# The last group of an encoder layer: low parts on VectorE, the second norm and the store batch by batch

## The chip, the core and the metric

The kernel runs on one core of one Trainium2 chip. The metric is the device time of a whole execution in microseconds, as the median of several runs. In the profile the engines are PE (TensorE, matmuls), PEld (its weight loads), DVE (VectorE), ACT (ScalarE), POOL (GpSimd) and SP (SyncE, which here only issues DMAs).

## What is computed

One transformer layer with cross attention, in float32, over 128 sequences of 128 tokens and 256 features:

```python
q, k, v = x @ Wq + bq, ctx @ Wk + bk, ctx @ Wv + bv        # 16 heads of 16
scores  = where(j < i, q k^T / 4, -1e30)
attn    = softmax(scores); attn[query 0] = 0
x   = layer_norm(x + (attn v) @ Wo + bo, ln1_g, ln1_b)
out = layer_norm(x + relu(x @ W1 + b1) @ W2 + b2, ln2_g, ln2_b)   # W1: 256 x 1024, W2: 1024 x 256
```

## The kernel before

The 128 sequences are worked off in 64 groups of two (`NG` = 64, `GB` = 2), so a group has 256 tokens; the last one is group 63. Each float32 operand of a dense product is kept as two `float32r` parts: a high part, which ScalarE rounds off while it takes the result out of PSUM, and a low part, the float32 value less the high part. A product is then three matmuls (`SPLIT`: high by high, high by low, low by high) into one PSUM bank.

Every engine runs a program written by hand: a function `iteration(it)` lists its steps, and each step carries the group that it belongs to at that point (`h_lo(it - 3, 0)`). It is called for `it` from -5 to 69, so several groups are in work at once, and steps of groups that don't exist fall away (`exists`). Engines meet only in semaphores; within an engine the order is the order of the code. Nothing else plans the work.

In the last iterations only the feed-forward half of group 63 is left. It goes as follows.

- TensorE, `ff_up(g, n)` for n = 0 to 3 (lines 439 to 443, `columns_product`, line 377): 12 matmuls each, giving 256 of the 1024 hidden features. The matmuls of n = 2 use the PSUM bank of n = 0 and wait until VectorE has taken that.
- ScalarE, `h_hi(g, n)` (line 660): relu with bias, rounded, into `hT[:, 0]`, in two instructions.
- VectorE, `h_full(g, n)` (line 866): the same relu in full float32 into `h_f32[:, n % 2]`, also in two instructions. It waits until the low part of n - 2 has been made, as there are two buffers.
- GpSimd, `h_lo(g, n)` (line 1014): `hT[:, 1]` = `h_f32` - `hT[:, 0]`, 128x512.
- TensorE, `ff_down(g, q)` for q = 0 to 3 (lines 445 to 457, `tokens_product`, line 387): 12 matmuls each; q = 0 and 1 are batches 0 and 1 over the first four chunks of hidden features, q = 2 and 3 over the last four. Both batches lie in one bank (`f2`, 512 columns). The first half waits for the low parts of n = 0 and 1, the second for 2 and 3.
- VectorE, `norm2_sum` (line 920, result plus `y_b2`, the residual), `norm2_stats` (line 882), `norm2_moments` (lines 888 to 892: mean and variance, `var_eps`, `neg_mean`).
- GpSimd, `rstd2` (lines 1050 and 1052): the reciprocal root and the offset, on two columns.
- ScalarE, `norm2` (line 678, in `standardise`): `u2 * rstd + offset`, one instruction per batch.
- GpSimd, `scale_z2` (line 1058, times the row `g2_row`, which waits for both batches) and `offset_z2` (line 1063, plus `be2_row`), both 128x512 in `o_tok`.
- SyncE, `store` (line 291): one DMA of 256 KB per group.

`y_b2` of group 63 is made by GpSimd in `scale_z1` (line 1037) and `offset_z1` (line 1044). In GpSimd's last iterations these steps stand between others of group 62: `rstd2` and `scale_z2` of group 62, `offset_z1` of 63, `offset_z2` of 62, `rstd2` of 63.

Of the kernel before, what the change touches and what calls it, by code (L numbers as in the profile page):

```python
# [7 lines left out]
ALU = mybir.AluOpType  # L8
# [31 lines left out]
def exists(g):  # L40

    return 0 <= g < NG
# [8 lines left out]
def encoder_layer(nc, x, ctx_in, Wq, bq, Wk, bk, Wv, bv, Wo, bo, ln1_g, ln1_b, W1, b1, W2, b2, ln2_g, ln2_b, out):  # L51
    ctx = ExitStack()
    with ctx:
# [138 lines left out]
        s_o = sem("o_ready")  # L192
        s_out = sem("out_stored")

        def f32(ap):

            return ap.bitcast(F32)

        WEIGHTS = [(Wq, wq, KC, D), (Wk, wk, KC, D), (Wv, wv, KC, D), (Wo, wo, KC, D), (W1, w1, KC, FF),
# [30 lines left out]
        def _(sp):  # L230
# [57 lines left out]
            def store(g):  # L288
                if exists(g):
                    sp.wait_ge(s_o, g + 1)  # L290
                    sp.dma_start(out_v[g], o_tok[:]).then_inc(s_out, 16)
# [41 lines left out]
            for it in ITERATIONS:  # L333
                iteration(it)
            sp.wait_ge(s_out, 16 * NG)


        @block.tensor
        def _(pe):
# [41 lines left out]

            def tokens_product(name, w, acts, b, kcs, total, starts=True):


                for kc in kcs:
                    for n, (a, c) in enumerate(SPLIT):
                        last = nc.tensor.matmul(ps_dense[BANK[name]][:, b * D:(b + 1) * D],  # L387
                                                acts[:, a, kc, b * S:(b + 1) * S], w[:, c, kc, :],
                                                start=(starts and kc == 0 and n == 0),
                                                stop=(kc == total - 1 and n == len(SPLIT) - 1),  # L390
                                                skip_group_check=True)
                return last
# [52 lines left out]
            def ff_down(g, q):  # L445
                if exists(g):
                    if q == 0:
                        weights_split(g, 5)
                        bank_free(g, "f2")
                    b, half = q % 2, q // 2  # L450
                    if b == 0:
                        pe.wait_ge(s_hlo[2 * half], g + 1)
                        pe.wait_ge(s_hlo[2 * half + 1], g + 1)
                    last = tokens_product("f2", w2, hT, b, range(4 * half, 4 * half + 4), FC,
                                          starts=(b == 0))
                    if q == 3:
                        last.then_inc(full["f2"], 1)
# [274 lines left out]
        def _(dve):  # L732
# [123 lines left out]
            def h_full(g, n):  # L856
                if exists(g):
# [7 lines left out]
                    for i in range(2):  # L865
                        last = nc.vector.tensor_scalar(  # L866
                            h_f32[:, n % 2, i, :], ps_dense[BANK[f"f1_{n}"]][:, i * GT:(i + 1) * GT],
                            b1_col[:, 2 * n + i:2 * n + i + 1], 0.0, ALU.add, ALU.max)
                    last.then_inc(taken[f"f1_{n}"], 1)

            def att_lo(g):
# [39 lines left out]
            def norm1_moments(g):  # L911
                if exists(g):
                    moments(0, g, s_st1, s_mv1, s_ve1, s_of1)

            def norm2_sum(g):
                if exists(g):
                    dve.wait_ge(full["f2"], g + 1)
# [6 lines left out]
            def norm2_stats(g):  # L924
                if exists(g):
                    statistics(1, u2, g, taken["f2"], s_st2)
# [52 lines left out]
            for it in ITERATIONS:  # L979
                iteration(it)  # L980


        @block.gpsimd
        def _(pool):
# [25 lines left out]
            def h_lo(g, n):  # L1010
                if exists(g):
                    pool.wait_ge(taken[f"f1_{n}"], g + 1)
# [41 lines left out]
            def scale_z2(g):  # L1054
                if exists(g):
                    pool.wait_ge(s_z2, GB * (g + 1))
                    need(pool, s_out, 16 * g)
                    nc.gpsimd.tensor_tensor(o_tok[:], u2[:], row(g2_row), ALU.mult).then_inc(s_og, 1)

            def offset_z2(g):  # L1060
                if exists(g):
                    pool.wait_ge(s_og, g + 1)
# [52 lines left out]
```

## Time and profile before

| | us |
|---|---|
| median of 3 runs (lowest, highest) | 1667.87 (1667.69, 1668.47) |
| the profiled execution | 1669.3 |
| its span in the trace | 1667.4 |
| busy in the span: PE | 1619.5 (97%) |
| PEld | 1592.4 (95%) |
| ACT | 1549.0 (93%) |
| DVE | 1432.2 (86%) |
| POOL | 1386.5 (83%) |

TensorE is busy nearly all the time. The groups repeat with a period of some 25 us, and the profile's picture in 40 slices shows full slices for all engines but the first and the last. In the last slice PE falls to 7 tenths, VectorE to 4 and ScalarE to 3. How the last stretch runs is read from the rows further down.

### The profile page before, as it was taken

The numbers are of one execution on the slowest core, as the hardware profiler recorded it, in microseconds if no ns is written. First come the engines' busy times: TensorE is split into PE (matmuls) and PEld (weight loads), VectorE is DVE, ScalarE is ACT, GpSimd is POOL, SyncE is SP. The second block draws the span as 40 slices with busy tenths as digits, with TensorE's granted clock in tenths as the row PEclk, the third lists the DMA queues.
The fourth block names the chain that finished last, engine by engine and source line by source line (L and its number), as shares of the span: only waits on it lengthen the run. The fifth ranks groups of instructions, "written<-read, shape, count | busy, mean of one in ns | idle before, by whom it ended". The sixth has DMA issues, their size and how long they took to land.

```text
span 1667.4 us, 54091 instructions
## 1 busy us (share of the span) xinstructions
PE 1619.5 (97%) x16700; PEld 1592.4 (95%) x16700; DVE 1432.2 (86%) x6735; ACT 1549.0 (93%) x5907; POOL 1386.5 (83%) x1358
## 2 busy tenths in 40 slices
PE   4799999999999999999999999999999999999997
PEld 3699999999999999999999999999999999999996
DVE  3688898898898898898898898898898889889874
ACT  3799999999999999999999999999999999999993
POOL 2368888888888888888888888888888888888896
PEclk7799999999999999999999999999999999999999
DMA  7856656656666655665665665665665665665520
GB/s 146 174 118 123 131 134 121 131 126 127 133 135 116 135 133 117 136 134 120 132 137 117 132 134 121 135 131 126 127 134 126 128 130 128 127 130 130 112 60 27
DMA packets 307071, 208.99 MB, mean 125 GB/s; under 512 B 164320, under 2 KB 281952, under 8 KB 306784
## 3 DMA queue, kind: packets, MB, share of 16 engines
q1 hardware_dynamic: 305088, 204.60, 59.6%
q8 instruction: 136, 2.23, 0.6%
q14 instruction: 151, 1.24, 0.3%
q10 hardware_dynamic: 1696, 0.92, 0.3%
HBM read 104.73 MB, written 50.33 MB: 93 GB/s over the span
## 4 chain that ended last, share of the span: by engine, by line
PE 94%; DMA 1%; SPq 1%; DVE 1%; ACT 1%; issue 1%; POOL 1%; POOLq 0%; ACTq 0%; DVEq 0%
PE ps_dense L377 32%; PE ps_dense L387 32%; PE ps_probsT L480 14%; PE ps_scores L470 7%; PE ps_att L498 7%; PE ps_dense L359 2%; ACT probs L575 0%; DMA k_spill<-kT 0%; SPq L278 0%; DMA k_stack<-k_spill 0%; POOL hT L1014 0%; DMA probs<-in_L_xattn_Wk_dram 0%; SPq L235 0%; DMA q_stack<-qT 0%; SPq L241 0%
## 5 line engine op out<-in xcount | busy, mean ns | idle before, releaser
L575 ACT ACTIVATE probs<-ps_scores,negmax 128x128 f32<-128x128 f32 x2048 | 744.2, 413 | 8.4 <-DVE negmax L782 5.0
L1006 POOL TENSOR_TENSOR probs<-probs,recip 128x512 f32<-128x512 f32 x512 | 534.2, 1044 | 136.7 <-DVE recip L765 136.5
L782 DVE CUSTOM_DVE_ANT_0 ps_scores<-ps_scores,mask 128x128 f32<-128x128 f32 x2048 | 527.6, 319 | 71.8 <-PE ps_scores L470 69.6
L575 ACT ACTIVATION_READ_ACCUMULATOR probs<-ps_scores,negmax 128x1 f32 x2048 | 517.4, 253 | 0.0
L387 PE MATMUL ps_dense<-w,hT 128*128 128x256 f32 x3072 | 420.9, 286 | 1.8 <-DVE u L903 0.9
L377 PE MATMUL ps_dense<-zT,w 128*128 128x256 f32 x3072 | 416.9, 285 | 0.5 <-DVE h_f L866 0.5
L1014 POOL TENSOR_TENSOR hT<-h_f,hT 128x512 fp32r<-128x512 f32 x256 | 327.6, 1294 | 93.3 <-DVE h_f L866 93.3
L377 PEld LDWEIGHTS ps_dense<-zT,w 128*128 128x128 f32 x3072 | 381.8, 189 | 0.9 <-issue 0.9
L387 PEld LDWEIGHTS ps_dense<-w,hT 128*128 128x128 f32 x3072 | 380.3, 188 | 2.3 <-issue 1.2
L592 ACT ACTIVATE probsT<-ps_probsT 128x508 f32<-128x508 f32 x512 | 319.2, 623 | 40.3 <-PE ps_probsT L480 40.1
L480 PE MATMUL ps_probsT<-ident,probs 128*128 128x128 f32 x2048 | 314.9, 276 | 0.0
L782 DVE DVE_READ_ACCUMULATOR2_ANT negmax<- 128x1 f32 x2048 | 287.1, 140 | 0.0
L480 PEld LDWEIGHTS ps_probsT<-ident,probs 128*128 128x128 f32 x2048 | 237.6, 141 | 12.7 <-issue 12.7
L470 PE MATMUL ps_scores<-k_stack,q_stack 96*128 96x256 f32 x1024 | 211.4, 288 | 21.9 <-ACT probs L575 14.1
L660 ACT ACTIVATE hT<-ps_dense,b_col 128x256 fp32r<-128x256 f32 x512 | 219.1, 492 | 13.7 <-PE ps_dense L377 9.9
L866 DVE TENSOR_SCALAR h_f<-ps_dense,b_col 128x256 f32<-128x256 f32 x512 | 222.9, 476 | 9.0 <-ACT hT L660 5.5
L470 PEld LDWEIGHTS ps_scores<-k_stack,q_stack 96*128 96x128 f32 x1024 | 161.0, 193 | 24.7 <-ACT probs L575 14.4
L678 ACT ACTIVATE u<-u,offset,rstd 128x256 f32<-128x256 f32 x256 | 150.2, 683 | 11.6 <-POOL offset L1052 8.2
L498 PE MATMUL ps_att<-probsT,v_sb 128*32 128x128 f32 x4096 | 126.8, 276 | 0.4 <-ACT probsT L592 0.4
L498 PEld LDWEIGHTS ps_att<-probsT,v_sb 128*32 128x32 f32 x4096 | 109.1, 111 | 9.4 <-ACT probsT L592 0.7
L377 PE MATMUL ps_dense<-xT,wq 128*128 128x256 f32 x756 | 104.8, 289 | 7.1 <-DVE xT L810 7.1
L1044 POOL TENSOR_TENSOR y_b<-y_b,be_row 128x512 f32<-128x512 f32 x64 | 108.8, 1700 | 0.0
(84 smaller groups left out, 2335.3 us busy)
## 6 DMA issues: line engine op xcount, KB each, us to landing
k_stack<-k_spill SPq DMA_DIRECT2D x384, 128.0 KB, 4.4
q_stack<-qT SPq DMA_DIRECT2D x762, 64.0 KB, 2.0
k_spill<-kT SPq DMA_DIRECT2D x128, 256.0 KB, 2.2
c_tok<-in_ctx_dram SPq DMA_DIRECT2D x256, 64.0 KB, 4.8
x_res<-in_x_dram SPq DMA_DIRECT2D x64, 256.0 KB, 3.1
out_dram<-o_tok SPq DMA_DIRECT2D x64, 256.0 KB, 2.8
x_tok<-in_x_dram SPq DMA_DIRECT2D x252, 64.0 KB, 2.4
probsT<-in_L_xattn_W_dram SPq DMA_DIRECT2D x1, 1024.0 KB, 11.1
```

The costliest lines, as they stand in the source:

```text
L377: last = nc.tensor.matmul(bank_of(name, g)[:, i * GT:(i + 1) * GT], w[:, a, kc, ch * P:(ch + 1) * P], acts[:, c, kc, :], start=(n == 0), s ...
L387: last = nc.tensor.matmul(ps_dense[BANK[name]][:, b * D:(b + 1) * D], acts[:, a, kc, b * S:(b + 1) * S], w[:, c, kc, :], start=(starts and ...
L470: last = nc.tensor.matmul(bank[:, 2 * i:2 * i + 2, :], q_stack[g % 2][:, j, c, b * S:(b + 1) * S], k_stack[g % 2][:, 4 * c + j, :, b * S:( ...
L480: last = nc.tensor.transpose(ps_probsT[m % 2][:, i, :], probs[:, m % 4, i, :], ident[:])
L498: last = nc.tensor.matmul(ps_att[32 * j:32 * j + 32, (c * GB + b) * S:(c * GB + b + 1) * S], v_sb[g % 2][:, b, 4 * c + j, e:e + 2, :], pro ...
L575: last = nc.scalar.activation(probs[:, m % 4, i, :], ps_scores[m % 2][:, i, :], ACT.Exp, bias=negmax[:, m % 4, i:i + 1], scale=-1.0, accum ...
L592: nc.scalar.activation(probsT[:, (g * UNITS + m) % NPT, :, 1:S], ps_probsT[m % 2][:, :, 1:S], ACT.Copy).then_inc(s_pTsb, 1)
L660: last = nc.scalar.activation(hT[:, 0, 2 * n + i, :], ps_dense[BANK[f"f1_{n}"]][:, i * GT:(i + 1) * GT], ACT.Relu, bias=b1_col[:, 2 * n + ...
L782: last = nc.vector.tensor_tensor_reduce(ps_scores[m % 2][:, i, :], ps_scores[m % 2][:, i, :], mask[:], -1.0, -MASKED, ALU.add, ALU.min, ac ...
L866: last = nc.vector.tensor_scalar(h_f32[:, n % 2, i, :], ps_dense[BANK[f"f1_{n}"]][:, i * GT:(i + 1) * GT], b1_col[:, 2 * n + i:2 * n + i + ...
L1006: nc.gpsimd.tensor_tensor(probs[:, m % 4], probs[:, m % 4], recip[:, m % 4, :].unsqueeze(2).broadcast_to([P, 4, S]), ALU.mult)\
L1014: nc.gpsimd.tensor_tensor(hT[:, 1, 2 * n:2 * n + 2, :], h_f32[:, n % 2], f32(hT[:, 0, 2 * n:2 * n + 2, :]), ALU.subtract).then_inc(s_hlo[n ...
```

## The change

Everything is tied to the last group (`g == NG - 1`); the other 63 are as before.

- `h_lo` of group 63 is dropped from GpSimd. In its place VectorE makes each low part right behind its `h_full`, after a wait on its own result (`taken[f1_n]`).
- The down product of batch 1 goes to a bank that the scores no longer need (`last_half`, the first half of `ps_scores[0]`); batch 0 stays. The order of the matmuls is unchanged. When batch 0 is complete (q = 2), a semaphore tells so.
- `last_sum` takes the place of `norm2_sum` and `norm2_stats`: sum and statistics of batch 0 on its own semaphore, then those of batch 1.
- `scale_z2` and `offset_z2` of group 63 are dropped from GpSimd. `last_out`, VectorE's last step, does both for each batch as that batch leaves ScalarE, again with a wait on its own result between the two.
- The store of group 63 is two DMAs of 128 KB, one per batch.

```diff
+        last_half = ps_scores[0][:, 0:2].rearrange("p h k -> p (h k)")
...
             def store(g):
-                if exists(g):
+                if g == NG - 1:
+                    for b in range(GB):
+                        sp.wait_ge(s_o, NG + b)
+                        sp.dma_start(out_v[g][:, b], o_tok[:, b]).then_inc(s_out, 16)
+                elif exists(g):
                     sp.wait_ge(s_o, g + 1)
                     sp.dma_start(out_v[g], o_tok[:]).then_inc(s_out, 16)
...
                     last = tokens_product("f2", w2, hT, b, range(4 * half, 4 * half + 4), FC,
-                                          starts=(b == 0))
+                                          starts=(b == 0 or g == NG - 1),
+                                          home=last_half if g == NG - 1 and b == 1 else None)
+                    if q == 2 and g == NG - 1:
+                        last.then_inc(s_first_half, 1)
...
                     last.then_inc(taken[f"f1_{n}"], 1)
+                    if g == NG - 1:
+                        dve.wait_ge(taken[f"f1_{n}"], g + 1)
+                        nc.vector.tensor_tensor(hT[:, 1, 2 * n:2 * n + 2, :], h_f32[:, n % 2],
+                                                f32(hT[:, 0, 2 * n:2 * n + 2, :]), ALU.subtract).then_inc(s_hlo[n], 1)
...
+            def last_sum():
+                g = NG - 1
+                dve.wait_ge(s_yb, g + 1)
+                need(dve, s_og, g)
+                for b, (s_full, count) in enumerate(((s_first_half, 1), (full["f2"], g + 1))):
+                    dve.wait_ge(s_full, count)
+                    nc.vector.tensor_tensor(u2[:, b, :], last_half if b else ps_dense[BANK["f2"]][:, 0:D], y_b2[:, b, :],
+                                            ALU.add).then_inc(s_sum0, 1)
+                    dve.wait_ge(s_sum0, b + 1)
+                    nc.vector.bn_stats(stats[:, 1, b, :], u2[:, b, :]).then_inc(s_st2, 1)
+
+            def last_out():
+                g = NG - 1
+                need(dve, s_out, 16 * g)
+                for b in range(GB):
+                    dve.wait_ge(s_z2, GB * g + b + 1)
+                    nc.vector.tensor_tensor(o_tok[:, b, :], u2[:, b, :], g2_row[:], ALU.mult).then_inc(s_last, 1)
+                    dve.wait_ge(s_last, b + 1)
+                    nc.vector.tensor_tensor(o_tok[:, b, :], o_tok[:, b, :], be2_row[:], ALU.add).then_inc(s_o, 1)
...
             def h_lo(g, n):
-                if exists(g):
+                if exists(g) and g < NG - 1:
...
             def scale_z2(g):
-                if exists(g):
+                if exists(g) and g < NG - 1:
...
             def offset_z2(g):
-                if exists(g):
+                if exists(g) and g < NG - 1:
```

What this moves is shown at three places. The rows name line, operation, output, inputs and shape, and in brackets the semaphores waited for (`h0_lo` is the low part of n = 0, `h0_hi` its high part, `f1_0_taken` the end of `h_f32` of n = 0). The line numbers of the changed kernel are higher. First VectorE in the up projection of group 63, from the moments of group 62 on, before:

```order
L888 BN_AGGR mv<-stats 128x2 [waits stats2_ready]
L888 BN_AGGR mv<-stats 128x2
L891 TENSOR_SCALAR var_eps<-mv 128x2 [waits offset2_ready,meanvar2_ready]
L892 TENSOR_SCALAR neg_mean<-mv 128x2
L866 TENSOR_SCALAR h_f<-ps_dense,b_col 128x256 [waits h3_lo,h1_hi]
L866 TENSOR_SCALAR h_f<-ps_dense,b_col 128x256
L866 TENSOR_SCALAR h_f<-ps_dense,b_col 128x256 [waits h0_lo,h2_hi]
L866 TENSOR_SCALAR h_f<-ps_dense,b_col 128x256
L866 TENSOR_SCALAR h_f<-ps_dense,b_col 128x256 [waits h1_lo,h3_hi]
L866 TENSOR_SCALAR h_f<-ps_dense,b_col 128x256
```

The same place after, from the moments' `var_eps` on:

```order
L905 BN_AGGR mv<-stats 128x2
L908 TENSOR_SCALAR var_eps<-mv 128x2 [waits offset2_ready,meanvar2_ready]
L909 TENSOR_SCALAR neg_mean<-mv 128x2
L879 TENSOR_SCALAR h_f<-ps_dense,b_col 128x256 [waits h3_lo,h1_hi]
L879 TENSOR_SCALAR h_f<-ps_dense,b_col 128x256
L885 TENSOR_TENSOR hT<-h_f,hT 128x512 [waits f1_1_taken]
L879 TENSOR_SCALAR h_f<-ps_dense,b_col 128x256 [waits h0_lo,h2_hi]
L879 TENSOR_SCALAR h_f<-ps_dense,b_col 128x256
L885 TENSOR_TENSOR hT<-h_f,hT 128x512 [waits f1_2_taken]
L879 TENSOR_SCALAR h_f<-ps_dense,b_col 128x256 [waits h1_lo,h3_hi]
L879 TENSOR_SCALAR h_f<-ps_dense,b_col 128x256
L885 TENSOR_TENSOR hT<-h_f,hT 128x512 [waits f1_3_taken]
```

A subtraction of 128x512 now follows each pair of relu instructions, and the next pair stands behind it.

Then VectorE from the down product of group 63 to its end, before:

```order
L920 TENSOR_TENSOR u<-ps_dense,y_b 128x512 [waits z2_scaled,y_b2_ready,f2_full]
L882 BN_STATS stats<-u 128x6 [waits f2_taken]
L882 BN_STATS stats<-u 128x6
L888 BN_AGGR mv<-stats 128x2 [waits stats2_ready]
L888 BN_AGGR mv<-stats 128x2
L891 TENSOR_SCALAR var_eps<-mv 128x2 [waits offset2_ready,meanvar2_ready]
L892 TENSOR_SCALAR neg_mean<-mv 128x2
```

and after:

```order
L938 TENSOR_TENSOR u<-ps_dense,y_b 128x256 [waits last_f2_first_batch_full,z2_scaled,y_b2_ready]
L941 BN_STATS stats<-u 128x6 [waits last_sum_first_batch]
L938 TENSOR_TENSOR u<-ps_scores,y_b 128x256 [waits f2_full]
L941 BN_STATS stats<-u 128x6 [waits last_sum_first_batch]
L905 BN_AGGR mv<-stats 128x2 [waits stats2_ready]
L905 BN_AGGR mv<-stats 128x2
L908 TENSOR_SCALAR var_eps<-mv 128x2 [waits offset2_ready,meanvar2_ready]
L909 TENSOR_SCALAR neg_mean<-mv 128x2
L948 TENSOR_TENSOR o_tok<-u,g_row 128x256 [waits z2_ready,out_stored]
L950 TENSOR_TENSOR o_tok<-o_tok,be_row 128x256 [waits last_scaled]
L948 TENSOR_TENSOR o_tok<-u,g_row 128x256 [waits z2_ready]
L950 TENSOR_TENSOR o_tok<-o_tok,be_row 128x256 [waits last_scaled]
```

One sum of 128x512 has become two of 128x256, each with its statistics, and four instructions with the rows stand at the end.

Last GpSimd from the second `h_lo` of group 63 to its end, before:

```order
L1014 TENSOR_TENSOR hT<-h_f,hT 128x512 [waits f2_full,f1_1_taken]
L1050 TENSOR_TENSOR rstd<-var_eps,neg_half 128x2 [waits z2_ready,var_eps2_ready]
L1052 TENSOR_TENSOR offset<-neg_mean,rstd 128x2 [waits rstd2_ready]
L1014 TENSOR_TENSOR hT<-h_f,hT 128x512 [waits f2_full,f1_2_taken]
L1014 TENSOR_TENSOR hT<-h_f,hT 128x512 [waits f2_full,f1_3_taken]
L1058 TENSOR_TENSOR o_tok<-u,g_row 128x512 [waits out_stored,z2_ready]
L1044 TENSOR_TENSOR y_b<-y_b,be_row 128x512 [waits z1_scaled]
L1063 TENSOR_TENSOR o_tok<-o_tok,be_row 128x512 [waits z2_scaled]
L1050 TENSOR_TENSOR rstd<-var_eps,neg_half 128x2 [waits z2_ready,var_eps2_ready]
L1052 TENSOR_TENSOR offset<-neg_mean,rstd 128x2 [waits rstd2_ready]
L1058 TENSOR_TENSOR o_tok<-u,g_row 128x512 [waits out_stored,z2_ready]
L1063 TENSOR_TENSOR o_tok<-o_tok,be_row 128x512 [waits z2_scaled]
```

and after, from the residual's scale (`y_b`) on:

```order
L1077 TENSOR_TENSOR y_b<-u,g_row 128x512 [waits f2_taken,z1_ready]
L1090 TENSOR_TENSOR rstd<-var_eps,neg_half 128x2 [waits z2_ready,var_eps2_ready]
L1092 TENSOR_TENSOR offset<-neg_mean,rstd 128x2 [waits rstd2_ready]
L1098 TENSOR_TENSOR o_tok<-u,g_row 128x512 [waits out_stored,z2_ready]
L1084 TENSOR_TENSOR y_b<-y_b,be_row 128x512 [waits z1_scaled]
L1103 TENSOR_TENSOR o_tok<-o_tok,be_row 128x512 [waits z2_scaled]
L1090 TENSOR_TENSOR rstd<-var_eps,neg_half 128x2 [waits z2_ready,var_eps2_ready]
L1092 TENSOR_TENSOR offset<-neg_mean,rstd 128x2 [waits rstd2_ready]
```

Between `rstd` of group 62 and `o_tok` of group 62 no `hT` is left, and behind the last `rstd` and `offset` nothing is.

## Rows read from the trace of the kernel before

**Rows 1.** Stretches: us, busy PE, PEld, DVE, ACT, POOL (instructions), PEclk, DMA share, GB/s.

```profile
1652.00:1658.00 6.00, 5.60 (x46) 5.23 (x44) 0.72 (x3) 1.09 (x2) 5.97 (x6) 1.00 0.02 4
...
1662.00:1663.00 1.00, 0.00 (x0) 0.00 (x0) 0.00 (x0) 0.20 (x1) 0.72 (x1) 0.50 0.00 0
```

**Rows 2.** Timeline, TensorE: start us, length us, line, operation, count, [idle before, releaser].

```profile
1641.39 3.10 PE L387 MATMUL ps_dense<-w,hT 128*128 128x256 f32 x24
1644.32 3.00 PE L377 MATMUL ps_dense<-zT,w 128*128 128x256 f32 x24
1647.84 3.08 PE L377 MATMUL ps_dense<-zT,w 128*128 128x256 f32 x24 [0.52 <-DVE h_f L866]
1651.44 3.08 PE L387 MATMUL ps_dense<-w,hT 128*128 128x256 f32 x24 [0.52 <-POOL hT L1014]
1654.86 3.09 PE L387 MATMUL ps_dense<-w,hT 128*128 128x256 f32 x24 [0.35 <-POOL hT L1014]
```

**Rows 3.** Timeline, GpSimd, the last group.

```profile
1647.77 1.29 POOL L1014 TENSOR_TENSOR hT<-h_f,hT 128x512 fp32r<-128x512 f32 x1 [1.13 <-DVE h_f L866]
...
1652.18 2.54 POOL L1014 TENSOR_TENSOR hT<-h_f,hT 128x512 fp32r<-128x512 f32 x2
1654.66 1.29 POOL L1058 TENSOR_TENSOR o_tok<-u,g_row 128x512 f32<-128x512 f32 x1
```

**Rows 4.** Timeline, VectorE, the same stretch.

```profile
1646.82 0.88 DVE L866 TENSOR_SCALAR h_f<-ps_dense,b_col 128x256 f32<-128x256 f32 x2 [0.82 <-ACT hT L660]
...
1647.88 1.20 DVE L891 TENSOR_SCALAR var_eps<-mv 128x2 f32<-128x2 f32 x1
...
1650.41 0.87 DVE L866 TENSOR_SCALAR h_f<-ps_dense,b_col 128x256 f32<-128x256 f32 x2 [0.48 <-ACT hT L660]
1651.83 0.88 DVE L866 TENSOR_SCALAR h_f<-ps_dense,b_col 128x256 f32<-128x256 f32 x2 [0.55 <-ACT hT L660]
```

**Rows 5.** The chain of waits behind the last matmul: start us, length us, what.

```profile
1657.98 0.70 DVE u L920
...
1658.71 0.77 DVE stats L882 x2
...
1661.11 0.60 ACT u L678
1661.71 0.50 ACTq L53
...
1662.28 1.26 POOL o_tok L1058
...
1663.58 1.30 POOLq L53
```

**Rows 6.** DMA from 1664 to 1668: GB/s in slices of 0.1 us; KB, us to landing.

```profile
GB/s 0 0 0 0 0 0 0 0 0 0 0 0 0 0 0 0 0 10 287 369 379 420 358 399 318 82 0 0 0 0 0 0 0 0 0 0 0 0 0 0
...
out_dram<-o_tok SPq DMA_DIRECT2D x1, 256.0 KB, 2.1
```

**Rows 7.** Groups by form, VectorE: shapes, count, busy us, mean ns.

```profile
L748 DVE TENSOR_TENSOR w<-o_tok,w 128x512 fp32r<-128x512 f32 x1 | 0.7, 678 | 0.0
...
L753 DVE TENSOR_TENSOR b_col<-ps_att,b_col 128x8 f32<-128x8 f32 x1 | 0.2, 166 | 1.4 <-PE ps_att L400 1.4
```

**Rows 8.** Timeline, VectorE and GpSimd around 1578 us.

```profile
1577.71 1.58 DVE L810 TENSOR_TENSOR cT<-c_flip,cT 128x512 fp32r<-128x512 f32 x1
...
1577.45 1.29 POOL L1044 TENSOR_TENSOR y_b<-y_b,be_row 128x512 f32<-128x512 f32 x1
1578.70 1.74 POOL L1063 TENSOR_TENSOR o_tok<-o_tok,be_row 128x512 f32<-128x512 f32 x1
```

**Rows 9.** Timeline, ScalarE, the last two groups.

```profile
1635.06 0.84 ACT L660 ACTIVATE hT<-ps_dense,b_col 128x256 fp32r<-128x256 f32 x2 [0.99 <-PE ps_dense L377]
1635.79 1.08 ACT L678 ACTIVATE u<-u,offset,rstd 128x256 f32<-128x256 f32 x2
...
1650.96 0.84 ACT L660 ACTIVATE hT<-ps_dense,b_col 128x256 fp32r<-128x256 f32 x2 [0.58 <-PE ps_dense L377]
```

More of the change, by code:

```diff
@@ L193, in encoder_layer @@
         s_out = sem("out_stored")
+        s_first_half = sem("last_f2_first_batch_full")
+        s_last = sem("last_scaled")
+        s_sum0 = sem("last_sum_first_batch")
         def f32(ap):
             return ap.bitcast(F32)
+        last_half = ps_scores[0][:, 0:2].rearrange("p h k -> p (h k)")
         WEIGHTS = [(Wq, wq, KC, D), (Wk, wk, KC, D), (Wv, wv, KC, D), (Wo, wo, KC, D), (W1, w1, KC, FF),
@@ L334, in _ @@
                 iteration(it)
-            sp.wait_ge(s_out, 16 * NG)
+            sp.wait_ge(s_out, 16 * (NG + 1))
         @block.tensor
@@ L380, in columns_product, with tokens_product @@
                 last.then_inc(full[name], 1)
-            def tokens_product(name, w, acts, b, kcs, total, starts=True):
+            def tokens_product(name, w, acts, b, kcs, total, starts=True, home=None):
+                home = ps_dense[BANK[name]][:, b * D:(b + 1) * D] if home is None else home
                 for kc in kcs:
                     for n, (a, c) in enumerate(SPLIT):
-                        last = nc.tensor.matmul(ps_dense[BANK[name]][:, b * D:(b + 1) * D],
+                        last = nc.tensor.matmul(home,
                                                 acts[:, a, kc, b * S:(b + 1) * S], w[:, c, kc, :],
@@ L913, in norm1_moments @@
                     moments(0, g, s_st1, s_mv1, s_ve1, s_of1)
+            def last_sum():
[16 more added lines that the diff above has]
+                    nc.vector.tensor_tensor(o_tok[:, b, :], o_tok[:, b, :], be2_row[:], ALU.add).then_inc(s_o, 1)
             def norm2_sum(g):
-                if exists(g):
+                if g == NG - 1:
+                    last_sum()
+                elif exists(g):
                     dve.wait_ge(full["f2"], g + 1)
@@ L980, in _ @@
                 iteration(it)
+            last_out()
         @block.gpsimd
@@ L1054, in scale_z2 @@
             def scale_z2(g):
-                if exists(g):
+                if exists(g) and g < NG - 1:
                     pool.wait_ge(s_z2, GB * (g + 1))
@@ L1060, in offset_z2 @@
             def offset_z2(g):
-                if exists(g):
+                if exists(g) and g < NG - 1:
                     pool.wait_ge(s_og, g + 1)
```

## The prediction

> **What bounds the kernel now.** The edit touches group 63 alone, so only the last 25 us count. I read the timeline of TensorE there first. It is busy at full clock until 1657.95 [rows 1, 2], with three gaps in the last group: one before the third product of the up projection, and one before each half of the down projection (`f2`). The last two are put down to GpSimd's `hT` (the low part of relu's output): 0.52 and 0.35 us by the view [rows 2]. Two runs of 24 matmuls without a gap start 2.93 us apart (1641.39 and 1644.32). By that pitch, 1647.84 + 2.93 = 1650.77 would do for the first half of `f2` instead of 1651.44. The second half starts at 1654.86, and without either gap would start at 1653.70. So **at most 1.16 us** can be won on TensorE, and for all of it both low parts of a half must be early enough.
>
> GpSimd is why they are not: its four `hT` take 1.29 us each, 1.24 to 1.25 apart when back to back, and the last ends at 1654.72 [rows 3]. On VectorE the `h_f` that feed them are done by 1652.71, and one of its instructions, `var_eps` on 2 columns, takes 1.20 us, starting 0.11 us after a GpSimd `hT` and ending with it [rows 3, 4].
>
> Behind TensorE all is serial, with nothing beside it. By the chain of waits [rows 5]: sum 0.70 from 1657.98, statistics 0.77, moments and the two small GpSimd steps, ScalarE from 1661.11 (0.60 + 0.50), GpSimd's scale from 1662.28 and its offset row to 1664.88, then the store, 2.1 us to landing [rows 6], and 0.4 us to the end of the span at 1667.4.
>
> **Part 1, the low parts on VectorE.** Four instructions of 128x512, two SBUF inputs, move. The weights' low parts have this shape and take 0.68 us [rows 7]; with the wait on VectorE's own result, 0.04 us (1658.68 to 1658.71 in rows 5), each adds 0.72 us to VectorE and takes 1.25 from GpSimd. VectorE then runs as follows. `h_f` of 0 starts at 1646.82 as before, its low part runs from 1647.74 to 1648.43. GpSimd has nothing to do there, so `var_eps` should cost 0.17 like its undisturbed instances, not 1.20, and `h_f` of 1 starts at 1648.77. Its low part is done at 1650.36, and TensorE needs it by 1650.6 (it starts 0.15 us after its releaser: 1647.69 to 1647.84 [rows 2, 4]): the first gap goes. `h_f` of 2 waits for ScalarE until 1650.41 as before; its low part ends at 1652.02; `h_f` of 3 follows in issue from 1651.94 to 1652.80, 0.09 us later than now [rows 4]. **The last low part starts at 1652.84** and, if nothing stands in its way, ends at 1653.53. With 0.15 us that is 1653.68, and TensorE is ready at 1653.70: the second gap goes as well, 1.16 us in all.
>
> What can stand in its way is the SBUF port. A VectorE subtraction of this shape that started 0.26 us after a GpSimd instruction took 1.58 us, not 0.68, and the GpSimd instruction after it took 1.74, not 1.29 [rows 8]: whoever comes second waits. By the Trainium skill ("SBUF — State Buffer", Who interferes with whom) a VectorE instruction with two SBUF inputs and a GpSimd one that reads SBUF exclude each other, and "whoever issues first gets the shared pair for the whole instruction"; the row agrees. Now GpSimd, freed of `hT`, has only `o_tok` of group 62 left to scale. It waits for ScalarE's second norm of group 62, which today waits for GpSimd's offset behind two `hT`. After the change that offset is early, so ScalarE goes on straight from `hT` of 3, which ends at 1651.80. At 1635.79 such a norm began 0.11 us before the `hT` ahead of it was out, and took 1.08 [rows 9]: 1651.69 to 1652.77, and with the 0.08 us of release from ScalarE to GpSimd (1662.21 to 1662.28 [rows 5]) GpSimd starts at **1652.85**. So the two meet within 0.01 us, less than I can work out. The side that wins decides the forecast.
>
> If VectorE wins, GpSimd's scale is put off by 0.5 us, and its offset row for `y_b2` of group 63, on which the new first sum waits, ends near 1655.9. TensorE ends the second half at 1654.86 - 1.16 + 3.09 = 1656.79.
>
> **Part 2, sum and statistics batch by batch.** The first batch's product is complete 12 matmuls (1.45 us) before the second's, in a bank of its own, so sum and statistics of batch 0 can run while TensorE works, at 1655.9 to 1656.8 behind `y_b2`. After TensorE's end one half remains. 128x256 is worked out from 128x512 (0.678) and 128x8 (0.166) [rows 7]: 0.166 + 248 x 1.016 ns = 0.42 us. So 0.42 + 0.04 + 0.42 + 0.04 = 0.92 us stand where 1.52 stood (1657.98 to the end of the statistics at 1659.48, and the 0.04): **0.60 us**. The two half products go into another bank in an order that is unchanged, at no cost. Moments, GpSimd's power and product and ScalarE are unchanged.
>
> **Part 3, scale and offset row on VectorE.** Now 1664.88 - 1662.21 = 2.67 us lie between ScalarE's end and the offset row's. After, batch 0 starts behind ScalarE's first instruction (1661.71): 0.03 + 0.42 + 0.04 + 0.42, then batch 1 overlaps by 0.08 in issue and takes 0.42 + 0.04 + 0.42: 1.71 us, to 1663.42 on the old scale, **1.46 us** sooner. GpSimd is idle by then, so nothing excludes VectorE.
>
> **Part 4, two stores of 128 KB.** The first is issued 0.8 us before the second, and SyncE needs 0.37 us for one, so it delays nothing. The last one moves half the bytes. 256 KB land in 2.1 us, of which their bytes move in some seven slices of 0.1 us at 320 to 420 GB/s and two at the edges, and the rest stands still [rows 6]. The bounds are 0 (if only the fixed part counts) and 0.4 us (half of the 0.8 in which bytes move); I take 0.3, nearer to the upper, since nothing else is moving then. The Trainium skill ("DMA: Bandwidth & Descriptors", Anatomy of one DMA) gives about 2.0 us fixed and bytes / 436e9 besides; 128 KB fewer would then be worth 0.3 as well.
>
> **The sum**, against the profiled span: 1.16 + 0.60 + 1.46 + 0.3 = 3.5 us, 1667.4 to 1663.9. That run took 1669.3, the median is 1667.87; taking the saving off the median gives **1664.4**. Bounds of the terms: TensorE 0 to 1.16, the batch split 0.4 to 0.65 (the second sum reads PSUM, whose 128x256 steps take up to 0.47), the row steps 1.3 to 1.55, the store 0 to 0.4.
>
> **Rivals.** (1) **GpSimd wins the port at 1652.85.** Its scale then runs to 1654.13; in rows 8 VectorE got in 0.14 us before the end by the view (1577.71 + 1.58 - 0.68 = 1578.61 against 1578.74), so the low part runs from 1653.99 to 1654.68 and TensorE starts at 1654.83, as now (1654.86). The TensorE term falls to nearly 0: 1.16 less, 2.4 in all, **1665.5**. This is the skill's rule named above, decided the other way. For it: any 0.02 us that I missed on VectorE's chain of nine steps. Against it: the same may be missed on ScalarE's side. (2) **The first half is not early.** If `y_b2` comes after 1656.4, since GpSimd was put off more than once, the first sum and statistics run into TensorE's end, and up to 0.6 us is lost: 1665.0. (3) **Slower:** VectorE's last low part is not let in between GpSimd's three back to back steps (scale, `y_b2` row, `o_tok` row, 1.24 us apart [rows 3]), and waits from 1652.84 to 1656.4. It then ends at 1657.1 and TensorE starts at 1657.3, 2.4 us later than now, which takes the other terms' 2.4. TensorE would by then have stood idle for 3.6 us. In the trace its granted clock was 1.00 until it ended and 0.50 (1.2 GHz of 2.4) in the stretch from 1662 to 1663, 4 us after its last matmul [rows 1]. If the clock fell in this wait too, the last 24 matmuls would take twice their 2.93 us: 2.9 more, and the small steps behind nothing, **1670.8**; with no gain on the store 1671.1, and the row steps at their upper bound bring it to 0.2% slower. It decides from a wait of some 3.6 us on; rows 8 speak against it, since there VectorE came in between two such steps. (4) The change does less than it says: stores of half the size land no sooner and the row steps take the upper bound; 0.45 less, 1664.8, at the edge of my forecast's range.
>
> **How the numbers follow.** A measurement of this kernel can tell about 0.2%, 3.3 us, from no change; the forecast of 3.5 stands just past it. Port won by VectorE, 0.47 (its own range 1664.0 to 1664.9; two thirds of it past the 0.2%). Port lost, 0.38. First half late, 0.11. Slower, 0.04, of which I count 0.03 past the 0.2%. So faster 0.34, within 0.2% 0.63, slower 0.03. The range: its low end is the won port with all bounds good (3.9) and 0.2 for the spread of medians, 1663.8; its high end the lost port without a gain on the store, 1665.8, with as much again for spread, 1666.2.
>
> **What would show it.** VectorE's four new subtractions at 0.68 to 0.70 us each, or the last at some 1.8; GpSimd's scale at 1.75 (won) or 1.28 (lost). TensorE's two `f2` runs 2.93 us apart without a gap, or the second still at 1654.8. `var_eps` of group 62 at 0.17. From TensorE's end to the last row step 6.9 us now, 4.8 after. The prediction is wrong if `var_eps` still takes over 1 us with GpSimd idle, if the first batch's statistics end after TensorE, or if the 128x256 steps take over 0.5 us.

## The result

| us | before | after |
|---|---|---|
| median of 15 runs each (lowest, highest) | 1668.48 (1667.50, 1671.08) | 1665.32 (1662.92, 1666.80) |
| profiled execution | 1669.3 | 1664.95 |
| its span | 1667.4 | 1663.1 |
| from the third up product of group 63 to the end of the span | 19.56 | 16.06 |

The ratio of the times is 0.9979, with a 95% interval of 0.9972 to 0.9985: 3.5 us faster by the ratio (2.5 to 4.7), 3.16 by the medians. The forecast was 3.5 us, as 1664.4; the measured 1665.32 is 0.9 above that and in the range. The ratio says 0.21%, with 0.15 to 0.28% by its interval: clear of no change, but on both sides of the 0.2% (3.3 us) that the prediction took as the least that can be told, so whether the gain is past that mark isn't settled. Of the 0.9, 0.6 are in the kernel before, whose median over 15 runs is 1668.48 where it was 1667.87 over 3.

The last row of the table is the measure that I use from here on. It runs from TensorE's start of the third up product of group 63 (1647.84 in [rows 2]) to the end of the span, covers everything that the edit touches, and leaves out what differs between two executions of one kernel (the last section). The two spans differ by 4.3 us, but 0.8 of that was there before the last group began: the third up product starts at 1647.04 in the changed kernel. What is left is 19.56 - 16.06 = 3.50 us.

Spans are printed to 0.1 us, so a time up to the end of the span is good to 0.05 us, and a difference of two to 0.1. Where less than that counts, I end at the last row step instead (the last instruction before the last store is issued), which the timeline gives to 0.01 us. Before, these lines bound the moments and the last row step of group 63:

```profile
1659.50 0.25 DVE L888 BATCH_NORM_AGGREGATE mv<-stats 128x2 f32<-128x6 f32 x2
...
1663.62 1.26 POOL L1063 TENSOR_TENSOR o_tok<-o_tok,be_row 128x512 f32<-128x512 f32 x1
```

So from the third up product to the end of the last row step it is 1664.88 - 1647.84 = 17.04 us before and 1660.90 - 1647.04 = 13.86 after: 3.18 us, and the remaining 0.3 to 0.4 are in the last store.

### The profile page after: what moved, and what is told of

It is laid out like the page before. It is cut to its first block, busy times and chain, and to the rows that moved or that the text cites. A ratio compares the mean times of both kernels' runs of the same rounds, so it can differ in the third digit from the quotient of the medians.

```text
span 1663.1 us, 54091 instructions
## 1 busy us (share of the span) xinstructions
PE 1622.1 (98%) x16700; PEld 1595.2 (96%) x16700; DVE 1434.9 (86%) x6744; ACT 1545.7 (93%) x5907; POOL 1379.0 (83%) x1352
## 4 chain that ended last, share of the span: by engine, by line
PE 95%; DVE 2%; ACT 1%; SPq 1%; DMA 1%; issue 1%; POOL 0%; POOLq 0%; ACTq 0%; DVEq 0%
PE ps_dense L386 32%; PE ps_dense L397 32%; PE ps_probsT L493 14%; PE ps_scores L483 7%; PE ps_att L511 7%; PE ps_dense L368 2%; ACT probs L588 0%; DVE ps_scores L795 0%; PE ps_att L410 0%; DMA probs<-in_L_xattn_Wk_dram 0%; DMA q_stack<-qT 0%; SPq L240 0%; SPq L246 0%; SPq L262 0%; SPq L283 0%
## 5 line engine op out<-in xcount | busy, mean ns | idle before, releaser
L1054 POOL TENSOR_TENSOR hT<-h_f,hT 128x512 fp32r<-128x512 f32 x252 | 321.2, 1284 | 90.3 <-DVE h_f L879 90.3
```

The source lines that it names most:

```text
L1054: nc.gpsimd.tensor_tensor(hT[:, 1, 2 * n:2 * n + 2, :], h_f32[:, n % 2], f32(hT[:, 0, 2 * n:2 * n + 2, :]), ALU.subtract).then_inc(s_hlo[n ...
```

## The profile after

TensorE's timeline of the changed kernel, which answers to [rows 2] (start us, length us, line, operation, count, idle before). Times are 0.80 us earlier than in the rows of before for the same event:

```profile
1643.52 3.00 PE L386 MATMUL ps_dense<-zT,w 128*128 128x256 f32 x24
1647.04 3.09 PE L386 MATMUL ps_dense<-zT,w 128*128 128x256 f32 x24 [0.52 <-DVE h_f L879]
1649.97 1.58 PE L397 MATMUL ps_dense<-w,hT 128*128 128x256 f32 x12
1651.39 1.58 PE L397 MATMUL ps_scores<-w,hT 128*128 128x256 f32 x12
1652.88 1.66 PE L397 MATMUL ps_dense<-w,hT 128*128 128x256 f32 x12
1654.38 1.58 PE L397 MATMUL ps_scores<-w,hT 128*128 128x256 f32 x12
```

Only the gap before the third up product is left. The second half of the down product starts 5.84 us after the third up product, not 7.02. GpSimd's and VectorE's timelines answer to [rows 3, 4]:

```profile
1648.91 0.70 POOL L1092 TENSOR_TENSOR offset<-neg_mean,rstd 128x2 f32<-128x2 f32 x1
1652.07 1.80 POOL L1098 TENSOR_TENSOR o_tok<-u,g_row 128x512 f32<-128x512 f32 x1 [2.46 <-ACT u L691]
1653.84 1.29 POOL L1084 TENSOR_TENSOR y_b<-y_b,be_row 128x512 f32<-128x512 f32 x1
1655.09 1.27 POOL L1103 TENSOR_TENSOR o_tok<-o_tok,be_row 128x512 f32<-128x512 f32 x1
```

```profile
1647.81 0.17 DVE L908 TENSOR_SCALAR var_eps<-mv 128x2 f32<-128x2 f32 x1
...
1650.52 0.69 DVE L885 TENSOR_TENSOR hT<-h_f,hT 128x512 fp32r<-128x512 f32 x1
...
1652.04 0.69 DVE L885 TENSOR_TENSOR hT<-h_f,hT 128x512 fp32r<-128x512 f32 x1
1655.16 0.42 DVE L938 TENSOR_TENSOR u<-ps_dense,y_b 128x256 f32<-128x256 f32 x1 [2.43 <-POOL y_b L1084]
1655.62 0.43 DVE L941 BATCH_NORM_STATS2 stats<-u 128x6 f32<-128x256 f32 x1
1656.00 0.42 DVE L938 TENSOR_TENSOR u<-ps_scores,y_b 128x256 f32<-128x256 f32 x1
1656.45 0.43 DVE L941 BATCH_NORM_STATS2 stats<-u 128x6 f32<-128x256 f32 x1
1656.92 0.25 DVE L905 BATCH_NORM_AGGREGATE mv<-stats 128x2 f32<-128x6 f32 x2
...
1660.48 0.42 DVE L950 TENSOR_TENSOR o_tok<-o_tok,be_row 128x256 f32<-128x256 f32 x1
```

The last low part (1652.04) started 0.03 us ahead of GpSimd's scale (1652.07) and took its plain 0.69; the scale took 1.80 instead of 1.28. `var_eps` takes 0.17. Last some pieces of the chain of waits from ScalarE's second norm of group 62 on, which answers to [rows 5], and the last two stores (KB, us to landing), which answer to [rows 6]:

```profile
1651.01 0.99 ACT u L691 x2
...
1652.07 1.80 POOL o_tok L1098
1653.87 1.26 POOL y_b L1084
...
1655.16 0.43 DVE u L938
...
1656.05 0.39 DVE u L938
...
1658.53 0.61 ACT u L691
...
1659.23 0.43 DVE o_tok L948
```

```profile
out_dram<-o_tok SPq DMA_DIRECT2D x2, 128.0 KB, 1.7
```

By this chain the bound no longer is TensorE but GpSimd's scale, which had to wait for the port, and the row for `y_b2` behind it. It is a tie: the second sum starts at 1656.00, and TensorE's last matmul ends at 1655.96 (before, the sum started 0.03 us behind that end).

## Experiments

All are read by the time from the third up product to the end of the span (19.56 us before, 16.06 after), and to the end of the last row step. A single execution stands behind each unless said otherwise. The theory is that of the prediction: the terms add up, and the port goes for a whole instruction to whoever is first. The rivals are named in the expectations. All times in one place:

| from the third up product, us | to the end of the span (to 0.05) | to the end of the last row step (to 0.01) |
|---|---|---|
| before | 19.56 | 17.04 |
| changed kernel | 16.06 | 13.86 |
| the same, second execution | 16.07 | 13.89 |
| low parts alone | 18.35 | 15.85 |
| rows and store alone | 17.82 | 15.62 |
| no split of the sum | 16.72 | 14.58 |
| one store | 16.40 | 13.87 |
| last low part late | 17.23 | 15.02 |
| row for `y_b2` early | 17.15 | 15.02 |
| turns made sure | 16.06 | 13.86 |
| turns made sure, low part late | 16.12 | 13.92 |
| batchwise | 15.15 | 12.98 |

### Each part by itself

The low parts alone, put into the kernel before:

```diff
                     last.then_inc(taken[f"f1_{n}"], 1)
+                    if g == NG - 1:
+                        dve.wait_ge(taken[f"f1_{n}"], g + 1)
+                        nc.vector.tensor_tensor(hT[:, 1, 2 * n:2 * n + 2, :], h_f32[:, n % 2],
+                                                f32(hT[:, 0, 2 * n:2 * n + 2, :]), ALU.subtract).then_inc(s_hlo[n], 1)
...
             def h_lo(g, n):
-                if exists(g):
+                if exists(g) and g < NG - 1:
```

> The kernel before with part 1 alone: the four low parts of group 63 on VectorE; sum, statistics, row steps and store as before. Measure for all runs here: from TensorE's start of the third up product of group 63 to the end of the span (19.56 us before, 16.06 in the changed kernel). Theory (the terms add up, TensorE's two gaps go): 18.4 us, the second half of the down product 5.85 us after the third up product instead of 7.02. Rival (the low parts gain nothing by themselves, since the sum would then wait for y_b2): 19.0 or more.

TensorE's timeline of this kernel:

```profile
1647.45 3.09 PE L377 MATMUL ps_dense<-zT,w 128*128 128x256 f32 x24 [0.52 <-DVE h_f L866]
1650.38 5.99 PE L387 MATMUL ps_dense<-w,hT 128*128 128x256 f32 x48
```

The span is 1665.8, so 18.35 us: 1.2 less than before, against 1.16 worked out. By the timeline the sum starts 8.96 us after the third up product (1656.41) where it was 10.14 before: 1.18 us, the same as in the changed kernel. All 48 matmuls of the down product run without a gap, so no wait is left there on TensorE.

Scale, offset row and store alone:

```diff
+                if g == NG - 1:
+                    for b in range(GB):
+                        sp.wait_ge(s_o, NG + b)
+                        sp.dma_start(out_v[g][:, b], o_tok[:, b]).then_inc(s_out, 16)
...
+            last_out()
...
             def scale_z2(g):
-                if exists(g):
+                if exists(g) and g < NG - 1:
...
             def offset_z2(g):
-                if exists(g):
+                if exists(g) and g < NG - 1:
```

> The kernel before with parts 3 and 4 alone: scale and offset row on VectorE per batch, two stores of 128 KB; low parts on GpSimd and sum as before. Theory: 1.40 us off the row steps and 0.32 off the store, 17.8 us from the third up product to the end. Rival (part of that gain comes from GpSimd having less to do earlier): 18.3 or more.

The span is 1663.6 with the third up product at 1645.78: 17.82 us, 1.7 less than before; 1.42 of it lies ahead of the end of the last row step (17.04 - 15.62), the rest in the store. TensorE keeps its two gaps here (0.50 and 0.34 us), and `var_eps` its 1.20, so nothing of this gain comes from an earlier place.

The changed kernel without the split of the sum:

```diff
-                                          starts=(b == 0 or g == NG - 1),
-                                          home=last_half if g == NG - 1 and b == 1 else None)
+                                          starts=(b == 0))
...
+                dve.wait_ge(full["f2"], g + 1)
+                nc.vector.tensor_tensor(u2[:].rearrange("p b d -> p (b d)"), ps_dense[BANK["f2"]][:],
+                                        y_b2[:].rearrange("p b d -> p (b d)"), ALU.add).then_inc(s_sum0, 1)
```

> The changed kernel with the sum and statistics of both batches again behind the whole down product, in one bank. Theory: 0.60 us longer than the changed kernel, 16.66 us. Rival (in the changed kernel the first sum waits for y_b2, and the split wins less than its halves say): 16.3.

The span is 1664.2 with the third up product at 1647.48: 16.72 us, 0.7 more (0.72 to the end of the last row step), where the rival expected about 0.3. From the sum's start to the moments it is 1658.06 - 1656.54 = 1.52 us against 0.92 in the changed kernel, the 0.60 of the prediction. Another 0.10 is that this sum starts 9.06 us after the third up product, where the low-parts-alone kernel and the changed kernel (its second sum) have 8.96. The chain of waits has a piece of VectorE's queue at the wait for TensorE, just ahead of the sum:

```profile
1656.45 0.05 DVEq L933
```

In this kernel that wait stands third in the code, behind those for `y_b2` and `o_tok`; in the low-parts-alone kernel it stands first, and the chain has no such piece. That the order of the waits costs the 0.1 us wasn't tried.

One store in place of two:

```diff
-                    for b in range(GB):
-                        sp.wait_ge(s_o, NG + b)
-                        sp.dma_start(out_v[g][:, b], o_tok[:, b]).then_inc(s_out, 16)
+                    sp.wait_ge(s_o, NG + GB - 1)
+                    sp.dma_start(out_v[g], o_tok[:]).then_inc(s_out, 16)
```

> The changed kernel with one store of 256 KB at the end in place of two of 128 KB. Theory (bytes of the last store count): 0.3 us longer, 16.4 us. Rival (landing is a fixed time): 16.1.

The DMA view of this kernel, for its last store (KB, us to landing):

```profile
out_dram<-o_tok SPq DMA_DIRECT2D x1, 256.0 KB, 2.1
```

2.1 us against 1.7. The span is 1662.9 with the third up product at 1646.50: 16.40 us, 0.3 more, with the last row step ended at 13.87 us as in the changed kernel (13.86), so all of it is in the store. So half the bytes are worth 0.3 to 0.4 us at this size, and landing is not a fixed time.

### Who is first at the port

The changed kernel with the last low part made late by a little:

```diff
                         dve.wait_ge(taken[f"f1_{n}"], g + 1)
+                        if n == 3:
+                            for i in range(3):
+                                nc.vector.memset(pad[:, 16 * i:16 * i + 16], 0.0)
```

> The changed kernel with three memsets of 16 columns on VectorE between the last relu and the last low part of group 63, so that this low part starts 0.1 to 0.2 us later, behind GpSimd's scale of group 62 instead of 0.03 us ahead of it. Theory (the port goes to whoever starts first, for the whole instruction): the low part takes 1.8 us instead of 0.69, GpSimd's scale 1.28 instead of 1.80, and the time from the third up product to the end is 17.2 us (16.06 in the changed kernel). Rival (the two share the port): no more than the memsets' own 0.1 to 0.2, 16.2.

VectorE and GpSimd in this kernel, and the second half of the down product:

```profile
1651.14 1.78 DVE L889 TENSOR_TENSOR hT<-h_f,hT 128x512 fp32r<-128x512 f32 x1
```

```profile
1651.09 1.28 POOL L1102 TENSOR_TENSOR o_tok<-u,g_row 128x512 f32<-128x512 f32 x1 [2.46 <-ACT u L692]
1652.33 1.73 POOL L1088 TENSOR_TENSOR y_b<-y_b,be_row 128x512 f32<-128x512 f32 x1
```

```profile
1646.07 3.09 PE L387 MATMUL ps_dense<-zT,w 128*128 128x256 f32 x24 [0.52 <-DVE h_f L880]
...
1653.06 1.66 PE L398 MATMUL ps_dense<-w,hT 128*128 128x256 f32 x12 [1.06 <-DVE hT L889]
```

The three memsets put the low part's start off by some 0.07 us (5.07 us after the third up product, 5.00 in the changed kernel), so that it comes 0.05 us behind GpSimd. It takes 1.78 instead of 0.69, GpSimd's scale 1.28 instead of 1.80, and the row after the scale now is the one held up (1.73). TensorE waits 1.06 us. The span is 1663.3: 17.23 us. To the end of the last row step it is 15.02 against 13.86: **1.16 more for a start 0.07 us later**. Sharing of the port is ruled out: in both kernels the one that starts first takes its plain time (VectorE 0.69, or GpSimd 1.28), and only the other is longer. This kernel is the rival "port lost" of the prediction, which gave 1.16 us.

The row for `y_b2` ahead of GpSimd's scale:

```diff
...
                 rstd2(it - 4)
+                if it - 4 == NG - 2:
+                    offset_z1(NG - 1)
```

> The changed kernel with GpSimd's offset row of the residual y_b2 of group 63 put ahead of its scale of group 62, since the chain of waits of the changed kernel runs through these two. Theory (port): the row now overlaps the low part of n = 2, which starts some 0.25 us late, the last low part then comes 0.25 us after GpSimd's scale and loses the port: 17.2 us. Rival (GpSimd's chain is what bounds, earlier y_b2 can only help): 15.9 to 16.05.

The last two low parts on VectorE in this kernel, and GpSimd's row and scale:

```profile
1651.14 0.88 DVE L885 TENSOR_TENSOR hT<-h_f,hT 128x512 fp32r<-128x512 f32 x1
...
1652.84 1.66 DVE L885 TENSOR_TENSOR hT<-h_f,hT 128x512 fp32r<-128x512 f32 x1
```

```profile
1650.18 1.29 POOL L1084 TENSOR_TENSOR y_b<-y_b,be_row 128x512 f32<-128x512 f32 x1
1652.67 1.28 POOL L1098 TENSOR_TENSOR o_tok<-u,g_row 128x512 f32<-128x512 f32 x1 [1.20 <-ACT u L691]
```

The chain of waits ran through this row, and having it earlier made the kernel slower: 1664.8 - 1647.65 = 17.15 us, and 15.02 to the end of the last row step, 1.16 more, as much as with the late low part. The row holds the port when the low part of n = 2 wants it (0.88 us instead of 0.69), the low part of n = 3 then comes 0.17 us after GpSimd's scale, and takes 1.66. A cause 0.19 us long was turned into 1.16 us by the next meeting.

Turns made sure: the row right behind the residual's scale, where GpSimd is idle, and the scale of group 62 behind the last low part.

```diff
...
                 scale_z1(it - 3)
+                if it - 3 == NG - 1:
+                    offset_z1(NG - 1)
...
                     need(pool, s_out, 16 * g)
+                    if g == NG - 2:
+                        pool.wait_ge(s_hlo[3], NG)
```

> The changed kernel with turns made sure: the residual's offset row right behind its scale, where GpSimd is idle, and GpSimd's scale of group 62 waits for the last low part. Theory: the chain through GpSimd is gone, TensorE's end bounds, which is within 0.04 us of it: 16.0 us. Rival (y_b2 held back more than that): 15.7.

VectorE from the last low part to the second sum:

```profile
1652.54 0.69 DVE L885 TENSOR_TENSOR hT<-h_f,hT 128x512 fp32r<-128x512 f32 x1
1655.18 0.42 DVE L938 TENSOR_TENSOR u<-ps_dense,y_b 128x256 f32<-128x256 f32 x1 [1.95 <-PE ps_dense L397]
1655.64 0.43 DVE L941 BATCH_NORM_STATS2 stats<-u 128x6 f32<-128x256 f32 x1
1656.50 0.42 DVE L938 TENSOR_TENSOR u<-ps_scores,y_b 128x256 f32<-128x256 f32 x1 [0.43 <-PE ps_scores L397]
```

The span is 1663.6: 16.06 us, and 13.86 to the end of the last row step, the same as the changed kernel; the 0.04 us hoped for didn't show. The first sum now starts when its product is complete, and VectorE stands idle before the second. So GpSimd's chain was not worth anything in the changed kernel: it tied with TensorE. One meeting is left here: the moved row ran from 1646.42 to 1647.69, and the low part of n = 0, started at 1647.43, took 0.81 us, not 0.69, in time that VectorE had to spare.

The same with the three memsets:

> The kernel with turns made sure, with the three memsets ahead of the last low part. Theory: the memsets cost only themselves, since nobody can take the port: 0.1 to 0.2 us more than without, 16.15 us, against 17.2 where the turns are left to chance. Rival (the delay of the low part costs 1.1 us whatever GpSimd does): 17.1.

The first two memsets and the last low part behind them:

```profile
1650.53 0.10 DVE L888 MEMSET pad<- 128x16 f32 x2
1650.56 0.67 DVE L889 TENSOR_TENSOR hT<-h_f,hT 128x512 fp32r<-128x512 f32 x1
```

The span is 1661.6 with the third up product at 1645.48: 16.12 us, 0.06 more than without the memsets (13.92 and 13.86 to the end of the last row step). So the memsets by themselves aren't the cause: the same small delay cost 1.16 us where the turns were left to chance.

### A version with one batch less at the end

On top of the turns, moments, reciprocal root, offset and ScalarE's norm go batch by batch too:

```diff
                     nc.vector.bn_stats(stats[:, 1, b, :], u2[:, b, :]).then_inc(s_st2, 1)
+                    dve.wait_ge(s_st2, GB * g + b + 1)
+                    nc.vector.bn_aggr(mv[:, 1, b, :], stats[:, 1, b, :]).then_inc(s_mv2, 1)
...
+                if g == NG - 1:
+                    for b in range(GB):
+                        pool.wait_ge(s_ve2, 2 * (g + b + 1))
...
                 need(dve, s_out, 16 * g)
+                dve.wait_ge(s_of2, g + GB)
```

> The kernel with turns made sure, and the moments, GpSimd's power and product and the norm also batch by batch: those of batch 0 run while TensorE still works on batch 1, and only one batch is left behind TensorE's end. VectorE's rows of batch 0 wait until GpSimd has made the offset of batch 1, so that they do not take its port. Theory: from the second sum to the last row step 4.1 us, not 4.9; 15.25 us from the third up product to the end, 0.8 less than the changed kernel, and 4.3 us (0.26%) below the kernel before. Rival (VectorE's extra instructions of batch 0 run into the second sum, or ScalarE's first norm does): 15.8 or more.

VectorE's two sums, and its first and last row steps:

```profile
1655.38 0.43 DVE L939 TENSOR_TENSOR u<-ps_dense,y_b 128x256 f32<-128x256 f32 x1 [1.94 <-PE ps_dense L397]
...
1656.71 0.42 DVE L939 TENSOR_TENSOR u<-ps_scores,y_b 128x256 f32<-128x256 f32 x1
...
1659.06 0.43 DVE L955 TENSOR_TENSOR o_tok<-u,g_row 128x256 f32<-128x256 f32 x1 [1.00 <-POOL offset L1100]
...
1660.31 0.42 DVE L957 TENSOR_TENSOR o_tok<-o_tok,be_row 128x256 f32<-128x256 f32 x1
```

The span is 1662.9 with the third up product at 1647.75: 15.15 us, 0.9 less than the changed kernel, and 0.88 less (12.98) to the end of the last row step. From the second sum (1656.71) to the end of the last row step (1660.73) it is 4.02 us against 4.90. The second sum starts 8.96 us after the third up product, as with the turns alone, so the extra steps of batch 0 hold nothing up, though only just: the last of them ends at 1656.73. In 11 runs its median is 1664.56 against 1667.94 of before (20 runs), ratio 0.9975 (0.9966 to 0.9984).

The changed kernel ran beside it:

> The changed kernel once more, on the same chip as the batchwise one and against the same runs of the kernel before. Theory: 3.5 us (0.21%) below the kernel before, 16.06 us from the third up product to the end, with the last low part again first at the port. Rival (the race of 0.03 us falls otherwise in another execution): 17.2 us, and a gain near 2.4 us.

Median 1665.07 in 11 runs, ratio 0.9979 (0.9970 to 0.9988). Its span is 1663.2 with the third up product at 1647.13, 16.07 us (13.89 to the end of the last row step), and the port was won again (low part at 1652.14, GpSimd's scale at 1652.16). By the times alone the batchwise version can't be told from the changed kernel, as their intervals overlap; by the traces, one of the batchwise version and two of the changed kernel, it is 0.9 us shorter.

## Why the prediction was right, point by point

| term | worked out | measured | from |
|---|---|---|---|
| gaps of TensorE | 1.16 | 1.18; 1.18 alone | 7.02 - 5.84 in the changed kernel; 10.14 - 8.96 with the low parts alone |
| sum and statistics split | 0.60 | 0.60 | 1659.50 - 1657.98 less 1656.92 - 1656.00; 0.72 when undone, 0.10 of it from a later start |
| row steps on VectorE | 1.46 | 1.40 | worked out below; 1.42 alone |
| smaller last store | 0.3 | 0.32, to 0.1 | 1667.4 - 1664.88 = 2.52 less 1663.1 - 1660.90 = 2.20; 0.3 when undone |
| sum | 3.5 | 3.50, to 0.1 | 19.56 - 16.06 |

- **The path of the low parts on VectorE** held to 0.03 us at every step. On the old scale (0.80 added) the low parts of n = 0, 2 and 3 start at 1647.73, 1651.32 and 1652.84, where the prediction had 1647.74, 1651.33 (from its end 1652.02) and 1652.84. `var_eps` fell to 0.17 as soon as GpSimd was idle.
- **The port** was the open question, at 0.47 to 0.38. It was worked out as 1652.84 against 1652.85 and came out as 1652.84 against 1652.87. A lead of 0.01 us can't be worked out from rows given to 0.01: the bracket that is cited for ScalarE's release (1662.21 to 1662.28) is 0.07, and with it in place of 0.08 the two would start together. So the mechanism and the price of each side were right, and that the forecast took the side that came true was luck. VectorE won in both profiled executions of the changed kernel, by 0.03 and 0.02 us, and in the low-parts-alone, no-split and one-store kernels too (GpSimd's scale took 1.81, 1.82 and 1.81 us there). That the lost port costs 1.16 us was shown with a delay of 0.07 us. That unprofiled executions win it as well is not shown by a trace; their ratio of 0.9979 is what a won port gives (0.9979 by 3.5 us) and a lost one would not reach (2.4 us, 0.9986, just outside the interval of the first 15 runs and inside that of the second 11).
- **Rival "first half not early"** was near. `y_b2` came at 1655.13 (1655.93 on the old scale, 1655.9 predicted), and the second sum started 0.04 us after TensorE's end. The split still gave its 0.6. One of the prediction's own signs of being wrong did come, though: the first batch's statistics ended at 1656.05, 0.09 us after TensorE's 1655.96. By the prediction's own figures, 1656.8 against 1656.79, that sign stood on the forecast itself. It did no harm: the second sum's recorded start, 1656.00, lies 0.05 us ahead of the end of these statistics and 0.04 behind TensorE's end, so nothing was left waiting.
- **Row steps.** From the moments' start to the end of the last offset row it is 1664.88 - 1659.50 = 5.38 us before and 1660.90 - 1656.92 = 3.98 after: 1.40. Nearly all of the 0.06 that is missing lies where ScalarE's first norm releases VectorE (its piece of the chain ends at 1658.53 + 0.61 = 1659.14, and VectorE starts at 1659.23: 0.09 us where I took 0.03); the 128x256 steps took 0.42 to 0.43 as worked out.
- **The store** landed in 1.7 us instead of 2.1. The price by bytes was about right: 0.32 by the printed spans, 0.38 by the spans as the trace files hold them (1667.415 and 1663.059), at the upper end of the stated 0 to 0.4. The seven slices in which bytes moved are at 287 to 420 GB/s, not 320 to 420. The Trainium skill ("DMA: Bandwidth & Descriptors", Anatomy of one DMA) describes DMAs that GpSimd issues; this store is issued by SyncE. Its bytes / 436e9 makes 0.3 us of 128 KB, an estimate, near the measured 0.3 to 0.4. Its fixed part of about 2.0 us would make 2.6 us of the 256 KB, and these landed in 2.1.
- **The slower rival** had nothing for it: GpSimd's three steps never held VectorE off twice, and TensorE's longest wait in the down product of any kernel here was 1.06 us, after which it went on at the same pace (1653.06 to 1654.56 for 12 matmuls, 1.50 us as in the changed kernel). What a wait of 3.6 us would have done to its clock no run here shows.
- **The distance of 0.9 us in the median** is not in the mechanism. 0.6 of it is the level of the kernel before (1667.87 over 3 runs, 1668.48 over 15), which I took from too few runs; the other 0.3 is the 3.16 us between the medians against 3.5, and both medians come from runs that spread over 3.6 and 3.9 us. The forecast stood 0.2 us past the 0.2% bound; the measured ratio of 0.21% stands on it.
- **A sum that was off.** From TensorE's end to the last row step the prediction said 6.9 us now and 4.8 after. By its own terms it is 6.93 - 0.60 - 1.46 = 4.87, and it came out as 1660.90 - 1655.96 = 4.94.

## What to carry to other kernels

In a serial tail the durations add up, so moving a step to the engine that has just made its input could be priced to 0.1 us here from rows of the same shape. Where the step has two SBUF inputs and moves to VectorE, look up what GpSimd starts within one instruction of it: a head start of 0.03 us decided over 1.16 us here, and a semaphore that fixed the order cost nothing that the trace shows. Don't pull an instruction forward because the chain of waits names it, before looking at whose port it will then take; the kernel with the early row lost 1.16 us that way.

## What the hardware showed that I had not expected

**Ahead of the last group, the profiled executions differ in their first 114 us only.** VectorE's first residual sum of the second norm started at these times in the kernel before and in the last kernel of the section on the port, turns made sure and memsets (duration ns, then first and last start us in the stretch):

```profile
L920 DVE TENSOR_TENSOR u<-ps_dense,y_b x2: 692/692/692, 114.0 to 138.9; 128x512 f32<-128x512 f32 x2
```

```profile
L963 DVE TENSOR_TENSOR u<-ps_dense,y_b x2: 692/692/692, 111.7 to 136.5; 128x512 f32<-128x512 f32 x2
```

Over the twelve profiled executions that start lies between 111.7 and 114.0 us, and the third up product of group 63 comes 1533.8 us later in each (1647.84 - 114.0 = 1533.8, 1645.48 - 111.7 = 1533.8). Read to 0.01 us by the timelines, the twelve distances lie between 1533.81 and 1533.83. Here are the engines in the stretches 0 to 110 and 110 to 1600 us (length, busy PE, PEld, DVE, ACT, POOL, PEclk, DMA share, GB/s) of the same two:

```profile
0.00:110.00 110.00, 74.25 (x568) 68.83 (x569) 65.13 (x299) 72.14 (x274) 43.46 (x48) 0.77 0.74 149
110.00:1600.00 1490.00, 1490.00 (x15585) 1470.12 (x15583) 1330.75 (x6294) 1439.33 (x5511) 1289.50 (x1259) 1.00 0.62 128
```

```profile
0.00:110.00 110.00, 74.94 (x589) 69.72 (x589) 67.56 (x308) 74.08 (x280) 45.79 (x49) 0.80 0.76 151
110.00:1600.00 1490.00, 1490.00 (x15584) 1470.11 (x15583) 1330.40 (x6292) 1439.47 (x5515) 1288.39 (x1260) 1.00 0.62 128
```

In the first stretch the mean granted clock is 0.77 and 0.80 (it was 0.74 to 0.80 over the twelve), in the second 1.00 in all. So in the first stretch TensorE is granted the lower of the two levels (1.2 GHz of 2.4) for part of the time, and it is busy for 74 to 80 of the 110 us. What decides how long this stretch takes was not tried. For an edit worth 3 us at the end, two profiles read from a mark behind the start are a better measure than two whole spans, since the starts alone differ by up to 2.4 us.

**A tiny GpSimd instruction can be held too.** The offset on two columns took 0.70 us in the changed kernel (1648.91), 0.20 before, as it met the low part of n = 1 on VectorE. It cost nothing there.
